# A decoder layer with attention, cross-attention and sixteen experts on one core: every place of the hand-written order redrawn

## What is computed

```python
# linear attention, 16 heads of 8 channels
q = gelu(x @ Wq.T + bq) + 0.21;  k = gelu(x @ Wk.T + bk) + 0.21;  v = x @ Wv.T + bv
z = 1 / (q . mean(k) + 1e-6);    kv = rope(k).T @ v / n;   out = (rope(q) @ kv) * z
x = layernorm(x + norm(out + x) * gamma + beta)
# cross-attention to a context of 77 rows, softmax over the 77
x = layernorm(x + softmax(Q @ K.T / sqrt(8)) @ V @ Wo + bo)
# 16 experts (128 -> 256 -> 128), weights of the top 4 of a softmax router, others 0
y = sum over e of c[:, e] * (gelu(x @ w1[e] + b1[e]) @ w2[e] + b2[e])
x = layernorm(x + y)
```

## Time and profile before

| | us |
|---|---|
| median of 3 runs (lowest, highest) | 672.42 (671.56, 672.63) |
| the profiled execution, its own time | 671.28 |
| its span, first to last instruction | 669.5 |
| PE busy in it | 597.3 (89%) |
| ACT busy | 424.4 (63%) |
| DVE busy | 419.7 (63%) |
| POOL busy | 241.4 (36%) |
| mean granted clock of TensorE, share of full | 0.934 |

### The profile page before, as it was taken

One profiled execution on the slowest core, in us unless ns is written; L12 is line 12 of the kernel. 1 busy time (PEld: TensorE's weight loads), 2 busy tenths in 40 slices (PEclk: granted clock), 3 DMA queues, 4 the chain that ended last, 5 costly groups with the idle time before them and its releaser, 6 DMA issues.

```text
span 669.5 us, 16331 instructions
## 1 busy us (share of the span) xinstructions
PE 597.3 (89%) x6356; PEld 439.3 (66%) x6356; DVE 419.7 (63%) x1435; ACT 424.4 (63%) x532; POOL 241.4 (36%) x162
## 2 busy tenths in 40 slices
PE   3635868979999999999999999999999999899993
PEld 2613754658776776777776877677776766586673
DVE  1354576636785678766885778577866785266444
ACT  2521726776558765795569755985598558955660
POOL 4540431433325422553225422643244332342331
PEclk9555679989999999999999999999998999999999
DMA  7340011000100021002100110002000100000000
GB/s 198 108 107 23 18 38 45 4 17 18 34 18 2 2 66 34 4 2 57 42 3 2 50 35 19 2 17 61 23 4 2 33 25 5 1 18 1 1 17 17
DMA packets 30309, 19.67 MB, mean 29 GB/s; under 512 B 4616, under 2 KB 28920, under 8 KB 30232
## 3 DMA queue, kind: packets, MB, share of 16 engines
q1 hardware_dynamic: 22664, 13.20, 7.2%
q10 hardware_dynamic: 7280, 5.01, 2.5%
q0 software_dynamic: 288, 0.42, 0.3%
HBM read 8.85 MB, written 2.10 MB: 16 GB/s over the span
## 4 chain that ended last, share of the span: by engine, by line
PE 67%; ACT 13%; issue 7%; DVE 4%; SPq 1%; ACTq 1%; DMA 0%; POOL 0%; POOLq 0%; DVEq 0%
PE ps L934 15%; PE ps L910 8%; PE ps L912 7%; PE ps L911 7%; PE ps L871 5%; ACT g L655 4%; PE ps L930 3%; ACT w_stage L618 3%; PE ps L932 3%; PE ps L931 3%; ACT L618 2%; ACT L655 2%; PE ps L724 2%; PE ps L834 2%; PE ps L779 1%
## 5 line engine op out<-in xcount | busy, mean ns | idle before, releaser
L478 POOL TENSOR_TENSOR gl<-g,gh 128x1024 f16<-128x1024 f32 x64 | 136.7, 2136 | 236.8 <-ACT gh L644 236.3
L655 ACT ACTIVATE g<-ps,b 128x512 f32<-128x512 f32 x256 | 167.7, 687 | 61.0 <-PE ps L912 59.5
L1237 DVE SCALAR_TENSOR_TENSOR acc<-ps,cw,acc 128x128 f32<-128x128 f32 x448 | 126.0, 344 | 107.0 <-PE ps L934 65.0
L934 PEld LDWEIGHTS ps<-w,g 128*128 128x128 f32 x1024 | 121.2, 192 | 15.7 <-issue 11.6
L934 PE MATMUL ps<-w,g 128*128 128x128 f32 x1024 | 127.5, 278 | 2.2 <-DVE acc L1237 2.0
L910 PE MATMUL ps<-x2h,w1h 128*128 128x512 f16 x256 | 98.9, 387 | 7.0 <-ACT g L655 6.0
L912 PE MATMUL ps<-x2h,w1l 128*128 128x512 f16 x256 | 98.5, 385 | 0.0
L911 PE MATMUL ps<-x2l,w1h 128*128 128x512 f16 x256 | 98.5, 385 | 0.0
L930 PE MATMUL ps<-w2h,gh 128*128 128x128 f16 x512 | 89.3, 219 | 1.7 <-DVE acc L1237 1.5
L932 PE MATMUL ps<-w2h,gl 128*128 128x128 f16 x512 | 89.0, 219 | 0.0
L931 PE MATMUL ps<-w2l,gh 128*128 128x128 f16 x512 | 89.0, 219 | 0.0
(11 more groups left out here) (161 smaller groups left out, 876.7 us busy)
## 6 DMA issues: line engine op xcount, KB each, us to landing
q_rep<-qx SPq DMA_DIRECT2D x90, 32.0 KB
x<-in_x SPq DMA_DIRECT2D x8, 256.0 KB, 3.3
w_stage<-in_L_ffn_w ACTq DMA_DIRECT2D x1, 2048.0 KB, 18.4
q_swap<-q SPq DMA_DIRECT2D x16, 128.0 KB, 2.1
out<-fin SPq DMA_DIRECT2D x8, 256.0 KB, 2.4
k_rep<-kx SPq DMA_DIRECT2D x96, 19.2 KB
cx<-in_ctx SPq DMA_DIRECT2D x8, 154.0 KB
w<-in_L_ffn_w ACTq DMA_DIRECT2D x2, 512.0 KB, 4.8
```

Of the source, the lines that this page charges most:

```text
L478: pool.tensor_tensor(gl[:, j % SPLIT_RING, :, :], g32[:, e % RING, :, :], gh[:, j % SPLIT_RING, :, :], ALU.subtract).then_inc(s["lo"], 1)
L655: act.activation(g32[:, e % RING, h, :], bH[:, h, :], ACT.Gelu, bias=b1[:, e, h:h + 1], scale=1.0 / WS).then_inc(s["gelu"], 1)
L934: m = pe.matmul(o, g32[:, e % RING, h, tok], w2[:, j, h, :], start=(h == 0), stop=(h == HALF - 1))
L1237: m = dve.scalar_tensor_tensor(out=(acc_all if e == E - 1 else acc)[:, b, :], in0=bY[:, b * P:(b + 1) * P], scalar=cw[:, b, e:e + 1], in1= ...
```

## The change

Only numbers in the tables change; the work, the functions and their number of calls stay. All twenty tables of the engines and all five lists of weight places are replaced. One of each as an example (the rest reads alike):

```diff
-ACT_AT = dict(x_t=0, q=2, kv23=12, cx_t=42, x1_t=51, k=50, q_x=58, max_t=17, scores_t=(27, 31, 37, 39), x2_t=63,
-              weights=2, c_t=58, gelu=1, high=3, u=(38, 42), ao_t=48)
+ACT_AT = dict(x_t=4, q=7, kv23=20, cx_t=46, x1_t=52, k=54, q_x=61, max_t=18, scores_t=(25, 38, 39, 40), x2_t=63,
+              weights=0, c_t=51, gelu=1, high=3, u=(40, 44), ao_t=50)
-LOAD_W = (22, 23, 44, 45)
+LOAD_W = (10, 42, 68, 70)
```

More of the change, by code:

```diff
@@ L79, in constants @@
     return np.ascontiguousarray(np.concatenate(list(cols.values()), axis=1), np.float32), where
-PE_AT = dict(x_t=1, q=4, kv01=6, kv23=9, k_mean=13, kv=28, den=33, out=33, cx_t=42, v1=44, x1_t=50, k=45,
-             q_x=60, scores=(8, 8, 10, 12, 12, 14, 15, 16), max_t=17, scores_t=(24, 28, 34, 40), values=(36, 37,
-             41, 42), wo=49, x2_t=63, logits=0, c_t=53, b2=62, first=3, next=0, second=0, u_t=(41, 44), ao_t=45)
-ACT_AT = dict(x_t=0, q=2, kv23=12, cx_t=42, x1_t=51, k=50, q_x=58, max_t=17, scores_t=(27, 31, 37, 39), x2_t=63,
-              weights=2, c_t=58, gelu=1, high=3, u=(38, 42), ao_t=48)
@@ L89 @@
[L89 to L124, removed]
-LOAD_W = (22, 23, 44, 45)
-ROWS_W = (8, 38)
+PE_AT = dict(x_t=3, q=5, kv01=11, kv23=16, k_mean=23, kv=28, den=30, out=36, cx_t=43, v1=47, x1_t=47, k=52,
+             q_x=60, scores=(7, 7, 8, 9, 10, 14, 15, 16), max_t=20, scores_t=(24, 30, 39, 40), values=(37, 40,
+             41, 42), wo=55, x2_t=62, logits=0, c_t=49, b2=63, first=3, next=0, second=0, u_t=(41, 47), ao_t=49)
@@ new lines @@
+ACT_AT = dict(x_t=4, q=7, kv23=20, cx_t=46, x1_t=52, k=54, q_x=61, max_t=18, scores_t=(25, 38, 39, 40), x2_t=63,
+              weights=0, c_t=51, gelu=1, high=3, u=(40, 44), ao_t=50)
+DVE_AT = dict(q=8, kv01=12, kv23=19, k_rot=22, k_mean=22, kv=25, den=33, out=35, norm1=37, norm2=37, x1=41,
+              v1=48, k=49, q_x=63, scores=(5, 5, 5, 9, 10, 13, 13, 13), max=15, pairs=(44, 46), wo=54, x2=57,
+              x2_t=61, logits=0, weights=2, cw=11, b2=62, combine=0, finish=30, q_sin=32, sums=19)
@@ new lines @@
+POOL_AT = dict(x_beta=19, k_rot=17, q_rot=26, res=27, norm1=35, norm2=35, x1=16, x2=59, finish=25, low=1)
+PE_FIRST = dict(x_t=0, q=0, kv01=0, cx_t=0, kv23=1, v1=33, k=37, k_mean=2, kv=10, den=36, out=51, x1_t=63,
+                q_x=63)
+PE_EARLY = dict(scores=(0, 0, 0, 0, 0, 0, 4, 5), max_t=7, scores_t=(10, 12, 33, 43), values=(17, 37, 45, 49),
+                u_t=(54, 55), ao_t=63, wo=63, x2_t=63)
+PE_ONE = dict(x_t=0, q=0, kv01=4, kv23=7, k_mean=8, kv=10, den=11, out=17, cx_t=54, v1=55, k=60, x1_t=60,
+              q_x=60)
@@ new lines @@
+PE_ZERO = dict(x_t=0, q=3, kv01=9, kv23=15, k_mean=24, kv=25, den=26, out=29, cx_t=41, v1=47, x1_t=45, k=49,
+               q_x=47, scores=(5, 7, 8, 8, 10, 10, 12, 13), max_t=18, scores_t=(24, 27, 32, 37), values=(31, 33,
+               39, 39), wo=54, x2_t=63, logits=0, c_t=58, b2=62, first=3, next=0, second=1, u_t=(39, 44),
+               ao_t=50)
+ACT_FIRST = dict(x_t=0, q=0, cx_t=11, kv23=23, k=47, x1_t=63, q_x=63)
+ACT_EARLY = dict(max_t=9, scores_t=(25, 29, 32, 42), u=(35, 44), ao_t=63, x2_t=63)
@@ new lines @@
+ACT_ONE = dict(x_t=0, q=2, kv23=8, cx_t=48, k=59, x1_t=52, q_x=60)
+ACT_ZERO = dict(x_t=0, q=1, kv23=19, cx_t=45, x1_t=46, k=51, q_x=48, max_t=20, scores_t=(29, 30, 35, 38),
+                x2_t=63, weights=1, c_t=61, gelu=3, high=3, u=(37, 39), ao_t=51)
+DVE_FIRST = dict(q=0, kv01=0, kv23=0, v1=21, k_rot=0, k_mean=0, q_sin=10, k=52, kv=17, den=27, out=42, norm1=59,
+                 norm2=62, x1=63, q_x=63)
+DVE_EARLY = dict(scores=(0, 0, 0, 0, 0, 0, 5, 6), max=11, pairs=(48, 52), wo=63, x2=63, x2_t=63)
@@ new lines @@
+DVE_ONE = dict(q=1, kv01=5, kv23=15, k_rot=22, k_mean=22, q_sin=27, kv=30, den=33, out=35, norm1=39, v1=50,
+               norm2=39, k=63, x1=48, q_x=57)
+DVE_ZERO = dict(q=0, kv01=11, kv23=14, k_rot=20, k_mean=21, kv=24, den=24, out=26, norm1=33, norm2=35, x1=38,
+                v1=42, k=51, q_x=53, scores=(6, 6, 6, 6, 7, 7, 10, 13), max=14, pairs=(46, 48), wo=56, x2=61,
+                x2_t=62, logits=0, weights=0, cw=10, b2=63, combine=1, finish=20, q_sin=17, sums=29)
+POOL_FIRST = dict(x_beta=23, k_rot=0, q_rot=16, res=41, norm1=53, norm2=62)
@@ L129, in build @@
+POOL_EARLY = dict(x1=29, x2=57)
+POOL_ONE = dict(x_beta=0, k_rot=10, q_rot=19, res=31, norm1=33, norm2=37)
+POOL_ZERO = dict(x_beta=18, k_rot=20, q_rot=15, res=21, norm1=34, norm2=34, x1=28, x2=57, finish=47, low=1)
+HIGH_W = (27, 33, 33, 57, 83, 114)
+LOW_W = (21, 36, 51, 71, 95, 101)
+SCALE_W = (48, 89)
+LOAD_W = (10, 42, 68, 70)
+ROWS_W = (25, 12)
 def build(nc, A, consts, where, out):
```

## The result

| | before | after |
|---|---|---|
| median (lowest, highest), us | 672.52 (671.56, 672.83) | 650.63 (647.70, 652.67) |
| the profiled execution's own time | 671.28 | 651.72 |
| its span | 669.5 | 649.6 |
| first logits of body 0 in it | 103.78 | 100.69 |

What follows compares the result with a forecast made beforehand. PE bounds the steady bodies; small cross-engine steps bound the lead-in. Lead-in -0.5, body 0 -5.0, body 1 -1.2, clock -1.5, steady bodies 0.0, body 6 -1.2, body 7 +0.3: 672.42 - 9.1 = 663.3 us (forecast 659.5 to 667.5; range 657 to 673).

Steps and rivals of the forecast that it cites:

- lead-in: Stretch before body 0: shorter x1 and sooner k rotation against later values' matmuls; 0.5 us gained, bounds 2.5 either way.
- body 0: First body: sooner score transfers and paired exponentials make 70 us of 75.2; 5.0 us gained, bounds 1.5 and 6.5.
- start of a body: Bodies 1 to 7: expert 13's combine behind the choice of experts, tanh ahead of the first gelu; 0.25 us lost each.
- copy of x2: Steady bodies: x2's copy now stands ahead of the bias matmuls (L898) in PE's list; 0.2 us gained each.
- body 6: Body 6: 2.56 us less on ACT, minus 1.2 us for transfers; 1.2 us gained, bounds -1 and 2.5.
- den: Steady bodies: L749 no longer right behind L743; of the 0.5 us wait for DVE's den 0.3 stays, 0.2 gained.
- transfer chain: SP's key and query transfers, kx to scores, at least 17.7 us; 0.3 us lost in bodies 1 to 5, 1.2 in body 6.
- tables (the gelu behind the exponential): ACT, steady bodies: two of six table changes go per group; 0.6 us wait gone, 0.1 back, 0.5 gained.
- small matmuls between large ones: PE, steady bodies: more scores' and values' matmuls entered behind L934, the dearer kind; 0.3 us lost, bounds 0 and 0.5.
- clock: TensorE half-clock stretches in two bodies, 1.5 us each, tied to L743 and den's wait; one expected to go, 1.5 us gained.
- handover: From body 0 to body 1: a late x2l no longer has another DVE step ahead of it; 1.2 us gained in body 1.
- the steady bodies gain too: Rival: transfers in time, den and gelu waits and both low clock stretches gone, -0.6 per body; 657.8 us, chance 0.10.

Runs made afterwards that it cites:

- start_old: Kernel after with earlier keys, POOL's addition for group 1 also waiting for x1, and the old order at a body's start; 0.9594 of the kernel before.
- keys_early: Kernel after with the keys' matmul (PE) and kx (ACT) sooner in the steady bodies; 0.9646 of the kernel before.
- exp_and_out: Kernel before with the steady bodies' exponentials, transposed scores and values at new places, den's matmuls sooner and the output's behind the next expert's first half; ratio 0.9798.
- exp_alone: Kernel before with only the steady bodies' transposed scores, exponentials, values and u at the places of the kernel after; ratio 0.9942.
- den_alone: Kernel before with only den's matmuls (L743) sooner in the steady bodies; ratio 0.9986.
- lead_only: Kernel before with only the lead-in's tables (order lists and weight places) of the kernel after; ratio 0.9952.
- zero_only: Kernel before with only body 0's tables (order lists) of the kernel after; ratio 0.9993.
- lead_zero: Kernel before with the tables (order lists) of both lead-in and body 0 of the kernel after; ratio 0.9847, 10.0 us faster.
- exp_spread: Kernel after with earlier keys and POOL's added wait for x1, but steady bodies' exponentials, transposed scores, values and u at old places; 1.0077 of the kernel before.

## Why the prediction missed

**Right.** The lead-in and body 0 as places of gain; the start of a body (0.25 forecast, 0.29 measured by start_old; the combine of expert 13 ended 3.85 us behind the logits, as computed); the copy of x2 ahead of L898 (0.2, and 0.22 in the step from the last `second` to the logits); body 6 (-1.2, and -1.5). For den too the working was near: "of the 0.5 us 0.3 stays", and some 0.2 stays. The walk of the transfer chain was right in its kind: from kx to the scores it was 17.99 us where they just did not wait and 18.9 where they waited 0.82, against 17.7 to 19.3 computed. (kx came 3.6 us later in the body, where I had 3.0, and PE asked for the scores 1.9 sooner, where I had 2.2.) Its price was low for the steady bodies: 1.5 us in bodies 1 to 5 together and 1.2 in body 6, against 2.5 and 0.9 in the first profile of the kernel after. The issues of the second spread took between 7.5 and 8.6 us there, as they had varied before. SP's issues around the start of its body 3:

```profile
298.39 7.54 SPq L306 DMA_DIRECT2D k_rep<-kx  x12
305.98 1.10 SPq L336 DMA_DIRECT2D q_rep<-zero_rows  x2
307.12 8.62 SPq L306 DMA_DIRECT2D q_rep<-qx  x12
```

**Wrong, and the largest part: the steady bodies.** Without the transfers they gain 1.88 us (71.32 to 69.44), where the terms of the forecast, without its 0.3 for transfers, made 0.35. Measured from the start of each group of matmuls to the start of the next, in body 3 of before and of keys_early, the terms are:

| term, us per body | forecast | measured |
|---|---|---|
| tables (the gelu behind the exponential) | 0.5 | 0.66 |
| den | 0.2 | 0.40 |
| copy of x2 | 0.2 | 0.22 |
| start of a body (start_old) | -0.25 | -0.29 |
| small matmuls between large ones | -0.3 | 0.9 (what is left) |

- *Small matmuls between large ones* is the step that failed: 1.2 of the 1.5 us that were missing in each body. I counted how often such a matmul comes behind a large one, and not what comes behind it. Of the 0.9 us, L738 and L749 have 0.3, the sixteen H together 0.5 and L934 0.2, and the rest is 0.1 longer. In exp_and_out, where only the exponentials, den and the output have moved, 0.65 of its 1.67 us are of this kind; exp_alone agrees, in that its waits are 1.66 us against 1.09 and its body is as long. Which neighbour each part has was not tried singly, and a part may be waits too short for the view. The plainest is L738: it took 1.09 us to the start of L848 behind it, and takes 0.90 to that of L934 in keys_early. PE before, and then in keys_early:

```profile
350.65 1.16 PE L738 MATMUL ps<-v,kr 128*128 128x128 f32 x8
351.74 0.42 PE L848 MATMUL ps<-q_rep,k_rep 32*77 32x128 f16 x16
```

```profile
333.21 1.05 PE L738 MATMUL ps<-v,kr 128*128 128x128 f32 x8
334.11 1.95 PE L934 MATMUL ps<-w,g 128*128 128x128 f32 x16
```

- *Tables and den* were sized at 0.7 and gave 1.06. The den wait is 0.62 us by the starts of the matmuls, not 0.5, of which 0.22 stays. That the two could be added is luck of this change, which moves L749 too: they lie beside one unbroken stretch of ACT, and exp_alone and den_alone, each with one of the two attacked, gained 0.00.

**Wrong: the clock.** I had two low stretches and expected one to go. Before there were three (one in body 0), and after none begins in bodies 0 to 6; the one that the lead-in ends with reaches 5.5 us into body 0. I tied them to L743 and den. In bodies 1 to 6 the profiles point to a wait for a gelu instead. In five profiles (before, lead_only, zero_only, lead_zero, exp_spread) eleven low stretches stand in these bodies, and each begins while an L910 waits 0.6 or 1.6 us for g, or within 1.0 us behind that wait, with another wait of PE some 2 us ahead. In bodies 1 to 6 of the thirteen other profiles there is none, also not in exp_alone and den_alone with their 1.2 and 1.3 us of wait for w_stage or den. This is no proof: no run changed the clock alone, 20 of the 31 bodies with such a pair of waits had no low stretch, and in body 0 the low stretches begin at other waits, such as those for w_stage (before, at 137.66) and for q_rep (den_alone, at 113.92). The cause stays open.

**Wrong: the lead-in**, -3.1 instead of -0.5. The copy x2h came at 99.33, where I had about 101, though x1 of group 0 was not 0.5 to 1.8 us shorter but 1.1 longer. The logits stand 1.36 us behind x2h and 3.78 before: L779 and L716 ahead of them, named in the prediction and given no number, were 2.4 us. The -3.1 is one pair of profiles: in the five with the old lead-in and body 0 the first logits stand at 101.31 to 104.64, in the eleven with the new ones at 97.22 to 100.69, 4.8 us sooner in the mean. And body 0 came out right in size (5.9 for 6.2) partly by luck. The 1.2 us of the handover, which the sum has under body 1, lie within the 75.2 us from logits to logits that body 0 was priced on, so they were counted twice; the walk alone said 70, and 69.33 was measured. The gain also rests on the new lead-in, as lead_zero shows.

The rival "the steady bodies gain too" was nearest in kind, at 657.8 and with a chance of 0.10. Even it gave a steady body only 0.6.

## What to carry to other kernels

Price a changed order from the start of each group of matmuls to the start of the next, and not from the list of waits alone: here some 0.8 of the 1.88 us that a steady body gained were in no wait that the view lists. Before crediting a single move for a wait, follow the engine that ends it backwards as far as it has no gap: removing a wait inside such a stretch gains nothing while the stretch stays. The places of the exponentials and of den's matmuls each measured as zero, and with the output's matmuls moved as well they gave 1.67 us a body, so try parts together where they share a stretch. When a new order takes the slack out of a transfer queue, look for the next small move that gives it back; here it was worth 4 us.
